# Causal mask by position on GpSimd, and three small pieces of the PEER stage moved off VectorE

## The reference, cut to what matters

```
# causal attention, 16 heads of width 16
scores = einsum('bhqd,bhkd->bhqk', Q, K) / sqrt(d)
scores = where(triu(ones((S, S)), k=1), -inf, scores)
probs  = softmax(scores)
out    = einsum('bhqk,bhkd->bhqd', probs, V)

# PEER, 8 heads, 64 + 64 keys, top 10
v1, i1 = top_k(s1, 10);  v2, i2 = top_k(s2, 10)
all_scores  = v1[..., :, None] + v2[..., None, :]
all_indices = i1[..., :, None] * 64 + i2[..., None, :]
vals, best  = top_k(all_scores, 10)
scores = softmax(vals)
h = gelu(einsum(x, W_down[expert])) * scores;  out = einsum(h, W_up[expert])
```

## Time and profile before

| | |
|---|---|
| median of three runs | 3894.4 us (3894.11 to 3904.38) |
| the profiled execution: its time | 3891.91 us |
| its span in the trace | 3889.9 us |
| PE matmul busy over the span | 3336.4 us (86%) |
| DVE busy | 2759.0 us (71%) |
| POOL busy | 1993.4 us (51%) |
| ACT busy | 1156.3 us (30%) |

### The profile page before, as it was taken

One profiled execution on the slowest core, in us unless ns is written; L12 is line 12 of the kernel. 1 busy time (PEld: TensorE's weight loads), 2 busy tenths in 40 slices (PEclk: granted clock), 3 DMA queues, 4 the chain that ended last, 5 costly groups with the idle time before them and its releaser, 6 DMA issues. The chain is left out here.

```text
span 3889.9 us, 93119 instructions
## 1 busy us (share of the span) xinstructions
PE 3336.4 (86%) x33694; PEld 2822.4 (73%) x33695; DVE 2759.0 (71%) x10928; ACT 1156.3 (30%) x2660; POOL 1993.4 (51%) x2200
## 2 busy tenths in 40 slices
PE   6999957875798998989999989878887888599998
PEld 4777735554688888888888888845564667599998
DVE  6666634556999999999999999768885443533333
ACT  1344435442222222222222222146663111122221
POOL 4444335540766666666666666768882000133332
PEclk8999969987899999999999999989997886699999
DMA  5444334442000000000000000045441002566665
GB/s 152 106 113 107 97 91 120 119 110 100 2 2 2 2 2 2 2 2 2 2 2 2 2 2 2 2 126 128 127 125 40 24 24 100 152 184 178 187 177 139
DMA packets 256102, 277.73 MB, mean 71 GB/s; under 512 B 44002, under 2 KB 200674, under 8 KB 255202
## 3 DMA queue, kind: packets, MB, share of 16 engines
q1 hardware_dynamic: 242081, 253.69, 22.8%
q0 software_dynamic: 13632, 18.91, 3.2%
HBM read 187.63 MB, written 72.29 MB: 67 GB/s over the span
## 5 line engine op out<-in xcount | busy, mean ns | idle before, releaser
L1163 POOL TENSOR_TENSOR peer_hot_v<-peer_hot_e,peer_parts 80x512 bf16<-80x512 bf16 x768 | 1045.0, 1386 | 456.4 <-DVE peer_hot_e L1202 443.2
L1008 PE MATMUL peer_ps_u<-peer_up,peer_g 128*128 128x256 f32 x2048 | 544.8, 414 | 0.6 <-DVE x_all L1319 0.6
L989 PEld LDWEIGHTS peer_ps_h<-peer_xnT,peer_down 128*128 128x128 f32 x4096 | 507.0, 195 | 17.0 <-DMA peer_down<-in_peer_down 2.5
L989 PE MATMUL peer_ps_h<-peer_xnT,peer_down 128*128 128x128 f32 x4096 | 506.9, 278 | 2.2 <-DMA peer_down<-in_peer_down 2.2
L999 PE MATMUL peer_ps_w<-peer_hot_v,peer_hot_u 80*128 80x32 bf16 x12288 | 347.7, 177 | 173.1 <-DVE peer_g L1214 111.7
L999 PEld LDWEIGHTS peer_ps_w<-peer_hot_v,peer_hot_u 80*128 80x128 bf16 x12288 | 336.5, 97 | 197.0 <-DVE peer_hot_u L1206 123.0
L1008 PEld LDWEIGHTS peer_ps_u<-peer_up,peer_g 128*128 128x128 f32 x2048 | 402.1, 206 | 56.7 <-issue 1.0
L1086 ACT ACTIVATE peer_g<-peer_ps_h 128x512 f32<-128x512 f32 x256 | 152.8, 597 | 904.8 <-PE peer_ps_h L989 904.7
L1206 DVE TENSOR_TENSOR peer_hot_u<-peer_count,peer_uvT 80x2048 bf16<-80x2048 bf16 x256 | 344.8, 1347 | 0.0
L2058 POOL DMA_INDIRECT moe_xg<-moe_xn_rows,moe_source x71 | 70.4, 991 | 420.7 <-DVE moe_target L2165 389.6
L2064 POOL DMA_INDIRECT out<-moe_y,moe_target x71 | 113.0, 1592 | 311.9 <-DVE moe_y L2195 308.9
(11 more groups left out here) (362 smaller groups left out, 6974.1 us busy)
## 6 DMA issues: line engine op xcount, KB each, us to landing
moe_w<-in_moe_w SPq DMA_DIRECT2D x142, 512.0 KB
causal_qs<-causal_qscratch SPq DMA_DIRECT2D x32, 384.0 KB, 3.9
cross_qs<-cross_qscratch SPq DMA_DIRECT2D x32, 384.0 KB, 3.7
band_qs<-band_qscratch SPq DMA_DIRECT2D x32, 384.0 KB, 4.0
moe_w<-in_moe_w SPq DMA_DIRECT2D x8, 1024.0 KB, 11.8
causal_qscratch<-causal_part SPq DMA_DIRECT2D x32, 192.0 KB, 2.6
causal_kscratch<-causal_part SPq DMA_DIRECT2D x32, 192.0 KB, 2.0
causal_ks<-causal_kscratch SPq DMA_DIRECT2D x32, 192.0 KB, 4.2
```

What stands on the lines that cost most here:

```text
L989: mm = nc.tensor.matmul(ps_h[:, n % 2, k * P:(k + 1) * P], down[:, c, 4 * n + k, :], xnT[:, par, c, :], start=(c == 0), stop=(c == DC - 1))
L1008: mm = nc.tensor.matmul(ps_u[:], g[:, par, v, :], up[:, v, :], start=(v == 0), stop=(v == EV - 1))
L1163: ins = nc.gpsimd.tensor_tensor(hot_v[0:SEL, n % RING, part], hot_e[0:SEL, n % RING], w, ALU.mult)
```

## The change

In the causal stage the table of -1e30 is kept for `find` alone. Its two matmuls of 128 columns become one of 256 columns, over both diagonal blocks of the bank. In `head` the mask matmuls go. GpSimd writes zeros above the diagonal into the two diagonal blocks of `probT` by position after the exponential (`factor`, one instruction a head), and `weigh` on TensorE waits for that and no longer for the exponential. In the PEER stage `norm` and `candidates` run on GpSimd, at the head of its macro step, and the sum of the exponentials is written by ScalarE as the accumulator output of eight exponentials of 10 columns, in place of one of 80 and a sum on VectorE.

```diff
             mask = sb("mask", [P, P], BF16)      # was [P, 2, P]
@@ attention_stage, Tensor.find
-                                              ks[0:ROWS, par, h, 0:n], start=True, stop=not rope)
-                        if rope:
-                            mm = nc.tensor.matmul(ps_1[:, h % 2, c0 + q * P:c0 + (q + 1) * P], ident16[:], mask[:, 0, :],
-                                                  start=False, stop=True)
+                                              ks[0:ROWS, par, h, 0:n], start=(not rope or q == 0), stop=not rope)
+                    if rope:
+                        diagonal = ps_1[:, h % 2, :].rearrange("p (n k) -> p n k", k=P)[:, 0:3:2, :]
+                        mm = nc.tensor.matmul(diagonal, ident16[:], mask[:].unsqueeze(1).broadcast_to((P, TT, P)),
+                                              start=False, stop=True)
@@ Tensor.head
-                                              qs[0:ROWS + 3, par, h, qfrom[k]:S], start=True, stop=not rope)
-                        if rope:
-                            mm = nc.tensor.matmul(ps_2[:, h % 2, c0:c0 + P], ident16[:], mask[:, 1, :],
-                                                  start=False, stop=True)
+                                              qs[0:ROWS + 3, par, h, qfrom[k]:S], start=True, stop=True)
@@ Tensor.weigh
+                    elif rope:
+                        pe.wait_ge(b_ready[0], HEADS * b + 4 * j + 4)
                     else:
                         pe.wait_ge(p_ready, HEADS * b + 4 * j + 4)
@@ Pool.factor
+                    if rope:
+                        pool.wait_ge(p_ready, HEADS * b + h + 1)
+                        e = probT[:, h, :].rearrange("p (n q) -> p n q", q=P)[:, 0:KT * TT - 1:2, :]
+                        nc.gpsimd.affine_select(e, e, [[0, KT], [1, P]], ALU.is_ge, 0.0, base=0,
+                                                channel_multiplier=-1).then_inc(b_ready[0], 1)
+                        return
@@ peer_stage, ScalarE
-                nc.scalar.activation(ew[:], ew[:], ACT.Exp).then_inc(exp_out, 1)
+                for h in range(NQ):
+                    ins = nc.scalar.activation(ew[:, h, :], ew[:, h, :], ACT.Exp, accum_out=es[:, h, :])
+                ins.then_inc(exp_out, 1)
@@ GpSimd: norm and candidates, as on VectorE before, with these calls
+            def candidates(t):
+                pool.wait_ge(halves_done, t + 1)
+                wait(pool, code_ready, t)
...
             def first():
+                pool.wait_ge(roots_ready, 1)
+                norm(0)
+                norm(1)
+                candidates(0)
...
             def macro(t, par):
+                if there(t + 2):
+                    norm(t + 2)
+                if there(t + 1):
+                    candidates(t + 1)
@@ VectorE: norm, candidates and their calls go; best_eight now waits
+            def best_eight(t):
                 dve.wait_ge(cand_ready, t + 1)
@@ choices
-                steps.link(nc.vector.tensor_reduce(es[:], ew[:], AX.X, ALU.add))
```

More of the change, by code:

```diff
@@ L1328, in first @@
             def first():
-                norm(0)
-                norm(1)
                 for a in range(0, 2 * NQ, 4):
                     halves(0, a, a + 4)
-                candidates(0)
-                best_eight()
+                best_eight(0)
                 next_eight()
@@ L1347, in macro @@
                     add(t - 2)
-                if there(t + 2):
-                    norm(t + 2)
                 for n in range(NCH):
@@ L1361, in macro @@
                     if there(t + 1):
[L1362 to L1363 removed]
                         if n == 1:
[L1365 removed]
+                            best_eight(t + 1)
                         if n == 2:
```

54 lines of the change are left out of this document (25 added, 29 removed).

## The result

The changed kernel takes 3867.6 us as the median of 4 runs (3862.8 to 3874.0), against 3896.7 (3894.1 to 3904.4) for the kernel before beside it: ratio 0.9923, interval 0.9902 to 0.9944, some 29 us faster. The forecast was 3874, with the causal stage 12 us slower and PEER 31 faster. The profiled execution took 3867.41 us, its span is 3865.4.

What follows compares the result with a forecast made beforehand. TensorE bounds the causal stage, with VectorE setting the pace in places; VectorE bounds PEER. From 3891.9 us: +12 causal, -31 PEER, +1.5 PEER's start gives 3874.4, forecast 3874; own range 3850 to 3895, whole range 3830 to 3918.

Steps and rivals of the forecast that it cites:

- PEER's start: Before the PEER loop nothing covers the moved work of tile 0: +1.5 us, once (0 to 4).
- Masks: Causal TensorE: fewer mask matmuls save 0.13 us a head, counting for 7 heads of 16: 0.9 us a sequence.
- The four places and 2.3 us a sequence: Causal stage: where TensorE's `find` weight loads waited for VectorE's maxima, behind `project` of s = 2 and s = 5.
- The wait: Causal `weigh` at s = 14 waits for GpSimd's selection of head 11, behind `turn_max` and the fourth `project`: 1.06 us a sequence.
- Contention: Causal stage: GpSimd's added load lengthens six pace-setting VectorE instructions by 0.1 us each: 0.6 us a sequence (0 to 1.5).
- half of that a time: PEER: VectorE's first one-hot pair each waits half a 0.4 us `candidates` add; with a `hot_v` shift, 0.5 us a tile.
- PEER tile of 47.4 us: Sign expected in the PEER stage: a tile of 47.4 us, from a profiled stretch of 48.4 and a net gain of 1.0.
- The page's view: PEER, skill page taken literally: VectorE's two instructions each wait out a small GpSimd one, 0.2 to 0.4 us; sum nearly unchanged.
- Exponentials: PEER on ScalarE: eight exponentials of 10 columns take 2.2 us in place of 0.27, ending before VectorE asks.
- All free: Rival: selection causes no wait and GpSimd's new work doesn't meet VectorE's; causal -15, PEER -45, 3832 us; chance 0.24.
- PEER's gain is eaten: Rival: `candidates` contends as `hot_v` does, 1.58 us for 1.50 saved; causal +12, total 3905; chance 0.15.
- GpSimd becomes the bound: Rival, causal stage: at 1.26 us a selection GpSimd needs 31.9 us a sequence, total 3917; chance 0.18.

Runs made afterwards that it cites:

- a3: Kernel before with the causal change but no GpSimd selection, second scores left unmasked, TensorE waiting for the exponential again; 3887.6 us.
- b1: Changed kernel with the three GpSimd instructions of the fourth `project` put behind the selection of head 11; 3853.4 us.
- a4: Kernel before with the causal change, but the selection on a tile nobody reads, second scores unmasked, TensorE waiting for the exponential; 3886.1 us.
- a1: Causal stage of the kernel before with the PEER stage of the changed kernel; 3857.1 us.
- c3: Kernel before with the causal change, but GpSimd fills 288 elements of its own tile with zeros in place of selecting, second scores unmasked; ratio 0.9995.
- b3: Kernel before with the PEER change alone, GpSimd's five `candidates` adds done twice, the second time on a tile of their own; 3917.5 us.
- b4: Kernel before with the PEER change alone, VectorE's one-hot pair of part 3 put behind `best_eight`; 3892.9 us.

## Why the prediction was right, step by step

The forecast's mechanisms are the ones in the traces, on both stages and with their signs. It gave 3874 and 3867.6 came; its range and its own case hold. Two things make its number look better than its terms. In the causal sum the masks were 0.26 us too good and the wait 0.45 too long, and the two errors offset. And the two stages came out 12 us better than forecast (3 and 9), of which 7 show against the profiled execution (3874.4 to 3867.4): the stretch behind the band stage, which the change does not touch, was 6.9 us longer in the trace after (918.3 for 911.4). Both are luck. The terms:

| term | forecast | measured |
|---|---|---|
| masks, a sequence | -0.9 | -0.64 (a3) |
| one selection | 0.55 us | 0.421 |
| TensorE's wait at s = 14 | +1.06 | +0.53 in the row, +0.61 by moving the split (b1) |
| GpSimd's work beside VectorE | +0.6 | +0.67 (a4's 0.40, and 0.27 more on `probT`) |
| a causal sequence | +0.75 | +0.64 |
| causal stage | +12 | +9.2 by its last addition |
| norm, candidates, sum leave VectorE | -1.50 a tile | -1.50 |
| comes back | +0.5 a tile | +0.15 by starts, +0.14 by a1's mean tile (48.85 to 47.48) |
| a PEER tile | -1.0 | -1.36 (48.79 to 47.43) |
| PEER's loop | -31 | -37.6 (a1), -40.0 (after) |
| PEER's start | +1.5 | +1.8 (cross stage's last to PEER's first addition, 166.8 to 168.6; 168.4 in c3, with PEER of before) |

*Masks.* "I count 7 heads of 16" was too many: 0.64 is 5 heads' worth. The four places and 2.3 us a sequence were waits of weight loads; only two of them reached the matmuls of `find`, with 0.9 us, and one the matmul that turns the maxima. A third in `find` appears once the masks are gone (247.52 in a3), and the one before `out` takes 0.38 us more, which is more than the two heads that I gave it. Taking work from TensorE lengthens the waits on VectorE and makes new ones.

*The wait.* Its place, its cause and its count were right. With 0.42 us a selection and the forecast's own sum it is 4 x 0.42 - 1.14 = 0.54, and the row has 0.53. The mis-sized term is its one unknown price, taken above the 0.40 that fixed part and elements gave, for the test of the position. The selection costs hardly more than that 0.40. That the sum then meets the row to 0.01 is in part chance: GpSimd's chain from the third `project` to the end of head 11 is 0.29 us longer than the sum (318.20 to 326.25), by the meeting in `turn_max`, and TensorE comes to `weigh` 0.35 later behind the third `project` than before, by its longer wait before `out`.

*Contention.* The size was right and the reason wrong. I had six instructions of VectorE at 0.1 us each, spread. In the trace it is two places: the two `norm`, 0.26 us longer (0.90 against 0.64), and one rotary sum, 0.56 longer (0.98 against 0.42). The second meets `turn_max`, which I had placed right in GpSimd's order for TensorE's sake without asking whom it would meet on VectorE.

*PEER.* The price that was too high is "half of that a time": 0.5 us was forecast to come back and 0.15 did. The meeting with short adds costs 0.15 and 0.11 us, and the later `hot_e` gains 0.58 because `candidates` now stands where `hot_v` stood. A later pair pays a part of it back. The price of `candidates` was a little high, 1.62 us alone where 1.9 was taken; its 2.79 in the loop is the meeting that the forecast charged to VectorE and that GpSimd pays. `norm` takes 1.2 where 0.5 was taken. Neither counted, since GpSimd had the room; b3 shows that 2.8 us more would have counted for half and more. `candidates` ends at 1704.94, and VectorE is in `hot_u` until 1707.21 before it can ask. The "PEER tile of 47.4 us" among the signs came true by chance: it was 1.0 off a stretch 0.4 short of a tile. And the 31 tiles were 28 at the full 1.4 us and three at nearly nothing.

*The page's view.* `hot_u` takes 2.06 us beside `hot_v` and 1.22 alone, 0.84 more, while a `hot_v` takes 7.20 / 6 = 1.20 there: at most one instruction of the other engine is waited for. The Trainium skill, "SBUF — State Buffer", section "Who interferes with whom", says of VectorE's two-port modes that whoever issues first keeps the shared ports for the whole instruction; carried over to two-input instructions, as the forecast did, the trace agrees, and so does the last add of `candidates`, which waits for a `hot_u` begun before it. That section also has VectorE's two-input instructions meet only what reads on GpSimd, and one-input ones in its two-port modes meet writes as well: the sum at 257.56 and the `norm` at 244.63 of c3 agree with both, though no row shows the mode of `norm`.

*Exponentials.* They take 1.66 us, not 2.2, and are covered by 4.5 us.

*The rivals.* "All free" (3832) fell on the causal side: both the wait and the load are there, as a3 and a4 show. On PEER's side it nearly held: -37.6 or -40 against -45. "PEER's gain is eaten" fell at the real price; b3, where the gain is more than gone, and b4, where a fifth of it is left, show two ways into it, and in both the meeting in `places` is a large part. "GpSimd becomes the bound" fell by the price of a selection: 0.42, not 1.05. The same section on pitfalls that the forecast named (the Trainium skill, "GPSIMD Engine Reference", "Performance pitfalls for Q7 kernels") was on the right side of this. The one-input `norm` at 1.2 us, beside a selection of the same 256 elements at 0.42, isn't explained by it.

## What to carry to other kernels

Work taken from an engine counts only in the places where that engine sets the pace, and its other waits grow by the rest: here 2.08 us of matmuls off TensorE gave 0.64. When work moves to an idle engine, walk its queue in order up to the instruction that someone waits for; the load (62%) said nothing, and one `project` ahead of one selection cost 0.6 us a sequence, which came back when its three instructions were moved behind. Even so the causal part only came out even (28.55 us against 28.52): what the masks gave, the meetings took. And ask of each instruction that the new work pushes back whom it will meet at its new place: a short neighbour cost VectorE 0.1 us here, a long one 0.5 to 0.8.

## What the runs showed of the hardware that I had not expected

- GpSimd's `tensor_scalar` with mean and rstd from memory, 128 x 256 f32, takes 1.2 us; VectorE took 0.32 by starts, and GpSimd's own two-input instruction of that size takes 0.67.
- GpSimd's selection by position, 128 x 256 f32 in place, takes 0.42 us, less than its two-input add and little more than a fill of 288 elements (0.336).
- An accumulator output on ScalarE is an instruction of its own, 0.19 us in the record and about 0.1 by starts.
- GpSimd's fill, which reads nothing, leaves VectorE's two-input sum at 0.41 us and makes a pair of `norm` 0.96 us long, where it takes 0.64 with nothing beside it and 0.73 to 0.90 beside selections, by how they fall.
- GpSimd's 8 x 256 split, 0.66 us alone, took 0.95 beside two of VectorE's sums, the second of which took 0.98 for 0.42: both engines paid, each in turn.
- Five short adds of GpSimd take 1.62 us alone and 2.79 when VectorE's `hot_u` begins ahead of the last: GpSimd waits for VectorE as VectorE does for it.
- VectorE's two-input instruction of 2240 elements in `places` takes 1.33 us alone and 2.09 beside `hot_v`, in all 28 tiles of b3 and b4 that were read.
- A part of 900 to 919 us behind the band stage differs between kernels that are the same there; what sets it stays open.
